# A four-layer graph network on one core: raw weight blocks loaded and turned first, and a landing wait inside the cell scatter

## The reference, cut to what matters

```python
# layer 0: mean of the neighbours, two 512x512 matrices, layernorm
h = x @ W_self.T + (segment_sum(x[src], dst) / deg) @ W_neigh.T + bias
# layer 1: two weighted graph convolutions (w = edge_weight, loops added)
# layer 2: a message per edge, then a GRU cell
m   = relu(concat(h[src], edge_attr) @ W1.T + b1) @ W2.T + b2
agg = segment_sum(m, dst)
gi, gh = agg @ W_ih.T + b_ih, h @ W_hh.T + b_hh      # 3 gates of 512 each
# layer 3: weighted sum of the neighbours, one matrix
x = x + segment_sum(h[src] * edge_w, dst) @ W.T + b
```

## Time and profile before

| | us |
|---|---|
| median of 3 runs | 1461.65 (1454.98 to 1465.86) |
| the profiled execution | 1465.06 |
| its span, first to last instruction | 1463.3 |
| first and last cell scatter issued on POOL | 42.82, 296.91 |
| PE: first transposes of the layer-0 tiles | 307.81 |
| SP: load of the sorted cells | 383.94 |
| PE: first matmul of the blocks | 391.82 |

### The profile page before, as it was taken

One profiled execution on the slowest core, in us unless ns is written; L12 is line 12 of the kernel. 1 busy time (PEld: TensorE's weight loads), 2 busy tenths in 40 slices (PEclk: granted clock), 3 DMA queues, 4 the chain that ended last, 5 costly groups with the idle time before them and its releaser, 6 DMA issues.

```text
span 1463.3 us, 20037 instructions
## 1 busy us (share of the span) xinstructions
PE 1204.0 (82%) x4298; PEld 748.8 (51%) x4298; DVE 1014.9 (69%) x2113; ACT 571.7 (39%) x1461; POOL 691.7 (47%) x760
## 2 busy tenths in 40 slices
PE   4410056579799999999999889999999999998998
PEld 1310023244344444455787655444444478887787
DVE  9750017645499999985237868888888889888543
ACT  0200011121377777022201128888887753334210
POOL 0577735710288888067667726666666500000000
PEclk9655568789899999999999999999999999999899
DMA  8811001511400000733422467777777600002220
GB/s 335 307 59 59 2 30 37 187 58 72 155 21 24 25 19 11 291 100 114 141 84 88 144 212 231 228 215 230 217 224 222 163 1 1 0 1 74 82 90 35
DMA packets 87258, 167.89 MB, mean 115 GB/s; under 512 B 16124, under 2 KB 44670, under 8 KB 84644
## 3 DMA queue, kind: packets, MB, share of 16 engines
q1 hardware_dynamic: 59588, 102.69, 20.8%
q0 software_dynamic: 25472, 59.97, 13.5%
q10 hardware_dynamic: 2144, 4.59, 1.0%
HBM read 115.96 MB, written 51.23 MB: 114 GB/s over the span
## 4 chain that ended last, share of the span: by engine, by line
PE 64%; DVE 12%; another core or an unknown queue 8%; issue 6%; DMA 3%; DVEq 2%; ACT 2%; POOL 2%; SPq 1%; ACTq 0%; POOLq 0%
PE pb L1328 10%; PE pb L1103 6%; PE pb L1228 6%; PE pb L1220 5%; PE pb L1423 5%; PE pb L1193 4%; PE pb L1396 4%; PE pb L1398 4%; PE pb L1397 4%; PE pb L1171 3%; PE pb L1342 3%; PE pb L1344 2%; PE pb L1345 2%; PE pb L1321 2%
## 5 line engine op out<-in xcount | busy, mean ns | idle before, releaser
L711 POOL DMA_INDIRECT cell_rows<-pay,idx x168 | 168.3, 1002 | 125.8 <-DVE idx L1569 74.5
L745 POOL DMA_INDIRECT dst_rows<-ering,gidx x168 | 172.4, 1026 | 100.8 <-issue 90.2
L1328 PE MATMUL pb<-arena 128*128 128x512 f32 x368 | 191.0, 602 | 13.0 <-ACT arena L970 12.5
L1113 PE MATMUL pb<-ident,arena 128*128 128x128 f32 x164 | 34.2, 382 | 132.6 <-issue 52.1
L799 POOL DMA_INDIRECT arena<-p_rows,arena x96 | 99.5, 1036 | 78.0 <-issue 26.9
L1897 DVE TENSOR_TENSOR arena<-pb,arena 128x512 f32<-128x512 f32 x184 | 122.1, 681 | 7.1 <-DMA arena<-p_rows,arena 3.7
L799 POOL DMA_INDIRECT arena<-p_rows,ws x88 | 92.6, 1052 | 50.7 <-issue 25.9
L1904 DVE SCALAR_TENSOR_TENSOR low<-arena,high 128x512 fp32r<-128x512 f32 x138 | 95.0, 688 | 29.2 <-ACT high L977 21.5
L855 ACT ACTIVATE arena<-iota,free 128x128 f32<-128x128 f32 x266 | 92.2, 394 | 53.3 <-PE pb L1193 39.5
L1540 DVE TENSOR_TENSOR arena<-pb,arena 128x505 f32<-128x505 f32 (+1 forms) x34 | 23.0, 677 | 126.3 <-remote 116.2
L813 ACT COPY ws<-pb 128x512 f32<-128x512 f32 x40 | 22.7, 589 | 224.5 <-remote 109.7
(11 more groups left out here) (329 smaller groups left out, 2663.0 us busy)
## 6 DMA issues: line engine op xcount, KB each, us to landing
dst_rows<-arena SPq DMA_DIRECT2D x6, 2046.0 KB, 17.5
ering<-in_edge_attr_dram SPq DMA_DIRECT2D x41, 256.0 KB
arena<-adj SPq DMA_DIRECT2D x10, 640.0 KB, 4.0
arena<-dst_rows SPq DMA_DIRECT2D x24, 264.0 KB
arena<-wt_gru SPq DMA_DIRECT2D x48, 128.0 KB
ws<-dst_rows SPq DMA_DIRECT2D x22, 264.0 KB
arena<-in_x_dram SPq DMA_DIRECT2D x18, 256.0 KB
arena<-in_L_gnn_W_hh_dram SPq DMA_DIRECT2D x3, 1024.0 KB
```

What stands on the lines that cost most here:

```text
L711: nc.gpsimd.indirect_dma_start(cell_rows[:, :], bass.IndirectOffsetOnAxis(idx1[:, j:j + 1], 0), pay1[:, j], None).then_inc(c_scattered[spa ...
L745: nc.gpsimd.indirect_dma_start(dst_rows[:, :], bass.IndirectOffsetOnAxis(gidx[:, k:k + 1], 0), ering[:, k, :], None).then_inc(e_scattered[ ...
L1328: nc.tensor.matmul(e_bank(k)[:], erowT[:, k % 4], w1e_sb, start=True, stop=True).then_inc(edge_mm, 1)
```

## The change

- SP loads the raw blocks before anything is zeroed. The zeros of `cell_rows` (two writes) follow the second block, those of `dst_rows` (24 writes of 512 KB instead of 6) follow the tenth. The zeros come from the edge ring `ering`, which DVE clears first (1056 elements a partition instead of 5120).
- The three turned "ih" blocks get places of their own (`ih_turned`) at the end of the adjacency area instead of sharing the ring `ws`. So PE turns all ten blocks first, between the counts and ranks, and multiplies in the second matrix (`fold`) after that. The x loads come behind all of it in SP's queue.
- In the cell scatter the first transfer of each span is issued as before; the second waits until all five transfers of the span before have landed. That is 33 added waits on POOL.
- DVE clears the adjacency area only after the last fold, and POOL and SP wait for the new counts of zero writes.

```diff
@@ -318,6 +319,12 @@
 
         ering_high = sb_under("ering_high", [P, 2, D], F32R)
         ering = sb("ering", [P, COL, EW])
+        zeros = ering[:].rearrange("p c w -> p (c w)")
+        CELL_ZEROS, DST_ZEROS = 2, 24
+        cell_zeros = (CELL_CHUNKS + SPARE) * 4 // CELL_ZEROS
+        dst_zeros = (DST_CHUNKS + SPARE) * EW // DST_ZEROS
+        assert max(cell_zeros, dst_zeros) <= COL * EW
+        assert cell_zeros * CELL_ZEROS == (CELL_CHUNKS + SPARE) * 4 and dst_zeros * DST_ZEROS == (DST_CHUNKS + SPARE) * EW
 
         assert over_rows + 9 * D <= vec2_start and low.shape[1] == (KT + 1) * D
         gru_high = [[ws_high[:, 0, k] for k in range(KT)],
...
@@ -452,6 +458,11 @@
         PARTS3 = numbered([("matrix", 0)] + [("row", k) for k in FIRST_ROWS] + [("matrix", 1), ("row", 9)]
                           + [("matrix", t) for t in range(2, NT)])
         wj = {b: A[("w", b, KT - 1 if b else 4)] + 1 for b in range(len(blocks))}
+        def turned_block(n):
+
+            name, third = blocks[n]
+            return ih_turned[:, third] if name[0:2] == "ih" else ws[:, n % 2]
+
         raw_src = {"w1h": w1_2, "ih0": w_ih, "ih1": w_ih, "ih2": w_ih, "hh0": w_hh, "hh1": w_hh,
                    "hh2": w_hh, "w3": w_3, "self": w_self, "neigh": w_neigh}
 
@@ -489,44 +500,40 @@
             column(wt_t, w_in, edges_loaded)
             column(w1t_t, w1_in.rearrange("e a -> (e a)"), edges_loaded)
 
-            sp.wait_ge(zero_ready, 1)
-            zc = (CELL_CHUNKS + SPARE) * 4
-            sp.dma_start(cell_rows.rearrange("(p c) w -> p (c w)", p=P), h.rearrange("p t d -> p (t d)")[:, 0:zc]).then_inc(cells_zeroed, 16)
-            for k in range(KT):
-                sp.dma_start(b2_col[:, k:k + 1], b2_2[k * P:(k + 1) * P].rearrange("(p a) -> p a", a=1)).then_inc(b2_loaded, 16)
-            zd = (DST_CHUNKS + SPARE) * EW
-            part = zd // 6
-            dz = dst_rows.rearrange("(p c) w -> p (c w)", p=P)
-            for k in range(6):
-                sp.dma_start(dz[:, k * part:(k + 1) * part], h.rearrange("p t d -> p (t d)")[:, 0:part]).then_inc(zeroed, 16)
-
             for n, (name, third) in enumerate(blocks):
-                if n == X_AFTER:
-                    sp.wait_ge(sorted_all, 1)
-                    sp.wait_ge(x_free, 1)
-                    for t in range(NT):
-                        m = P if t + 1 < NT else LAST
-                        sp.dma_start(xs[0:m, t], x_in[t * P:t * P + m, :]).then_inc(xe_loaded[t], 16)
                 if n >= 2:
                     sp.wait_ge(for_act, wj[n - 2])
                 wide = DE + D if name == "w1h" else D
                 raw = raw_src[name]
                 sp.dma_start(wst[:, n % 2, :, 0:wide],
                              raw[third * D:(third + 1) * D, :].rearrange("(o p) f -> p o f", p=P)).then_inc(raw_loaded[n % 2], 16)
-                if n == 3:
-                    sp.wait_ge(zeroed, 16 * 6)
+                if n == 1:
+                    sp.wait_ge(zero_ready, 1)
+                    cz = cell_rows.rearrange("(p c) w -> p (c w)", p=P)
+                    for k in range(CELL_ZEROS):
+                        sp.dma_start(cz[:, k * cell_zeros:(k + 1) * cell_zeros], zeros[:, 0:cell_zeros]).then_inc(cells_zeroed, 16)
+                    for k in range(KT):
+                        sp.dma_start(b2_col[:, k:k + 1], b2_2[k * P:(k + 1) * P].rearrange("(p a) -> p a", a=1)).then_inc(b2_loaded, 16)
+                if n == W2_AFTER:
                     sp.dma_start(w2_raw, w2_2.rearrange("(o p) f -> p o f", p=P)).then_inc(w2_loaded, 16)
                 if 1 <= n <= len(stored_blocks):
                     store_weights(sp, n - 1)
-                if n == len(blocks) - 1:
-                    sp.wait_ge(b2_ready, 1)
-                    for k, v in enumerate((b0, gamma0, beta0)):
-                        sp.dma_start(vec[:, k], v.rearrange("(a f) -> a f", a=1).to_broadcast([P, D])).then_inc(vec_loaded, 16)
-                if blocks[n - 2][0][0:2] == "ih":
-                    gate = blocks[n - 2][1]
-                    sp.wait_ge(act_read, A[("c", gate)] + 1)
-                    sp.dma_start(wt_dram[f"m{gate}"], m_out.rearrange("p k f -> p (k f)")).then_inc(m_stored, 16)
-                    sp.dma_start(c_dram[gate], c_out).then_inc(m_stored, 16)
+
+            dz = dst_rows.rearrange("(p c) w -> p (c w)", p=P)
+            for k in range(DST_ZEROS):
+                sp.dma_start(dz[:, k * dst_zeros:(k + 1) * dst_zeros], zeros[:, 0:dst_zeros]).then_inc(zeroed, 16)
+            sp.wait_ge(b2_ready, 1)
+            for k, v in enumerate((b0, gamma0, beta0)):
+                sp.dma_start(vec[:, k], v.rearrange("(a f) -> a f", a=1).to_broadcast([P, D])).then_inc(vec_loaded, 16)
+            for gate in range(3):
+                sp.wait_ge(act_read, A[("c", gate)] + 1)
+                sp.dma_start(wt_dram[f"m{gate}"], m_out.rearrange("p k f -> p (k f)")).then_inc(m_stored, 16)
+                sp.dma_start(c_dram[gate], c_out).then_inc(m_stored, 16)
+            sp.wait_ge(sorted_all, 1)
+            sp.wait_ge(x_free, 1)
+            for t in range(NT):
+                m = P if t + 1 < NT else LAST
+                sp.dma_start(xs[0:m, t], x_in[t * P:t * P + m, :]).then_inc(xe_loaded[t], 16)
 
             for t in range(1, NT + 2):
                 if t <= NT:
...
@@ -708,6 +717,9 @@
                 at_least(pool, c_scattered[span % 2], 16 * SPAN * (span // 2))
                 passed()
                 for j in range(SPAN * span, min(SPAN * span + SPAN, J)):
+                    if span and j == SPAN * span + 1:
+                        pool.wait_ge(c_scattered[(span - 1) % 2], 16 * SPAN * ((span + 1) // 2))
+                        passed()
                     nc.gpsimd.indirect_dma_start(cell_rows[:, :], bass.IndirectOffsetOnAxis(idx1[:, j:j + 1], 0),
                                                  pay1[:, j], None).then_inc(c_scattered[span % 2], 16)
 
...
@@ -822,26 +834,21 @@
             nc.scalar.copy(pay1[:, :, 3], w1t_t).then_inc(weights_copied, 1)
 
             for n in range(len(blocks)):
-                m = n - 2
-                if 0 <= m < len(stored_blocks):
+                m = {2: 0, 3: 1, 4: 2, 8: 4, 9: 3}.get(n)
+                if m is not None:
                     act.wait_ge(wt_stored[m % 2], 16 * (m // 2 + 1) + (16 if m % 2 == 0 else 0))
-                elif m >= 0:
-                    act.wait_ge(for_act, A[("c", blocks[m][1])] + 1)
-                if blocks[n][0] == "self":
-                    root(("he", 1), one_rstd[:])
                 for k in range(KT):
-                    copy_job(("w", n, k), ws[:, n % 2, k])
+                    copy_job(("w", n, k), turned_block(n)[:, k])
                 if n == 0:
                     copy_job(("w", 0, 4), tiles[:, 0])
-                if blocks[n][0] == "neigh":
-                    root(("he", 0), one_rstd[:])
-                if blocks[n - 1][0][0:2] == "ih":
-                    gate = blocks[n - 1][1]
-                    if gate:
-                        act.wait_ge(m_stored, 32 * gate)
-                    for k in range(KT):
-                        copy_job(("m", gate, k), m_out[:, k])
-                    copy_job(("c", gate), c_out)
+            for gate in range(3):
+                if gate:
+                    act.wait_ge(m_stored, 32 * gate)
+                for k in range(KT):
+                    copy_job(("m", gate, k), m_out[:, k])
+                copy_job(("c", gate), c_out)
+            root(("he", 0), one_rstd[:])
+            root(("he", 1), one_rstd[:])
 
             def flat(t4):
                 return t4.rearrange("p k n -> p (k n)")
@@ -1139,42 +1146,53 @@
                                            start=False, stop=g == last - 1)
                 ins.then_inc(for_dve, 1)
 
+            pe.wait_ge(const_ready, 8)
             pe.wait_ge(sort_const, 1)
             for q in range(len(O_PARTS) - 1):
+                if q < 2:
+                    turn_weights(q)
                 pe.wait_ge(hot1_ready, q + 1)
                 for g in range(O_PARTS[q], O_PARTS[q + 1]):
                     count_span(g)
-            pe.wait_ge(const_ready, 8)
+            turn_weights(2)
             pe.wait_ge(base_ready, 1)
-            for n in range(len(blocks)):
-                if n < 2:
-                    rank_spans(n)
-                elif n == 2:
-                    rank_spans(2)
-                    rank_spans(3)
-                elif n < 5:
-                    rank_spans(n + 1)
-                turn_weights(n)
-                if n == 6:
-                    rank_spans(6)
-                if blocks[n - 1][0][0:2] == "ih":
-
-                    gate = blocks[n - 1][1]
-                    pe.wait_ge(w2_loaded, 16)
-                    pe.wait_ge(b2_ready, 1)
-                    pe.wait_ge(act_read, wj[n - 1])
-                    for k in range(KT + 1):
-                        job = ("m", gate, k) if k < KT else ("c", gate)
```

(53 more changed lines are left out.)

22 lines of the change are left out of this document (11 added, 11 removed).

## The result

The changed kernel takes **1420.01 us** (median of 4, 1412.60 to 1420.17) against 1461.49 for the kernel before (4 runs), ratio 0.971, 95% interval 0.966 to 0.976. It is 41 us faster where 90 were forecast. The profiled execution took 1419.97, its span is 1418.2.

What follows compares the result with a forecast made beforehand. Bound: PE's late signals during POOL's unbroken cell scatter; afterwards the scatter itself. Scatter 257.7 + pauses 36 + handover 8 = 301.7 against 391.8, 90 us less, hence 1372 us; 8 in 10 for 1340 to 1430.

Steps and rivals of the forecast that it cites:

- These pauses ... let PE's signals through.: Cell scatter: pauses with no more than one transfer in flight let PE's signals through, as between edge scatters 1.52 us apart.
- Rival B: Pauses help halfway: PE gets one signal per span, about 7.3 us; tiles late, first matmul at 331, 1401 us; chance 12%.
- The main chain without late signals.: Sort, x load, layernorm, ten tiles: DVE's 86 us ends the sort near 129, PE starts about 157, chain ends near 231.
- The 33 pauses, 36 us.: POOL's landing waits: 6.4 pauses of 3.5 us under full DMA load plus 26.6 quiet ones of 0.5 us.
- The scatter as the bound at 294.: Cell scatter: 168 transfers at 1.287 us from 42.8 end at 257.7; with 36 us of pauses POOL stops near 294.
- Handover 8 us.: From the scatter's end through SP's load of the cells to the first block matmul: 6 plus 1.8 us for landing.
- Sum.: First block matmul at 257.7 + 36 + 8 = 301.7 against 391.8, 90 us less.
- Rival A: Zeros queued beside the scatter hold its landings, whole spans stand still: up to 22 us more, 1390 with 18; chance 12%.
- I take that as a fact of these rows: During a long unbroken scatter burst PE's signals reach the others late, about one in 11.1 us; mechanism left open.

Runs made afterwards that it cites:

- before_third: The kernel before, unchanged, run again in a session where PE's signals were prompt: 1324.98 us.
- after_third: The changed kernel, unchanged, run again in a session where PE's signals were prompt: 1370.59 us, ratio 1.033 to the kernel before.
- zeros_early: The changed kernel with its 24 zero writes right behind the column loads, in a session with prompt signals: 1377.20 us, ratio 1.035.
- order_only: The changed kernel without its landing wait, in a session with late signals: 1434.52 us, ratio 0.984 to the kernel before.
- gap_no_wait: The changed kernel with one small POOL memset per span in place of the landing wait, late signals: 1406.78 us, ratio 0.964.
- gap1: The changed kernel with one small POOL memset per span behind each landing wait, late signals: 1400.18 us, ratio 0.961.
- gap3_no_wait_b: The changed kernel with three POOL memsets per span in place of the landing wait, session with late signals: 1380.74 us, ratio 0.938.
- before_again: The kernel before, unchanged, run again in a later session with late signals: 1470.50 us.

## Why the prediction was wrong, step by step

- **"These pauses ... let PE's signals through."** This is the step that failed. It held for the sort (x at 140.79) and failed for the tiles. It rested on edge scatters 1.52 us apart, but the new quiet span takes 6.70 us, 1.34 per transfer, which is far nearer to the late 1.28 than to 1.52. The forecast's own figures, (6.43 + 0.5) / 5 = 1.39, already lay nearer to 1.28. The sort was saved by something else: beside the weight loads and zeros, until about 112 us, its pauses made spans of 10.9 to 13.5 us, 2.2 to 2.7 per transfer. Some 75 us after these ended the signals were late. The runs put 1.33 to 1.40 on the late side and 1.47 on the prompt side, and show that emptying the queue once in five transfers is not enough to let the signals through. Price: the first block matmul comes at 347.58 and not at the 313.20 of the same kernel with prompt signals, 34 us.
- **Rival B** comes nearest: the sort gets through and the tiles are late. Its price was too low (first matmul 331 for 347.6, 1401 for 1420). Its reason, "one signal per span", did not hold: the waits on remote grow from 3 to 41 us while the burst goes on.
- **The main chain without late signals.** x was forecast near 130 and is loaded at 140.79 (142.28 in before_third). DVE was taken as the bound with 86 us; from 45 to 141 us it is busy for 78. PE is busy for 75 of these 96 where 60 were counted, and ACT stands 18.47 and 5.04 us on "DMA c<-arena", the c store behind the 24 zero writes. With prompt signals the tiles are over at 254.18 in before_third and 244.66 in after_third, not at 231. None of this sets the end.
- **The 33 pauses, 36 us.** Measured 39: seven loaded ones with 32.5 us idle, less the usual 0.3 each, make 30.4 (22.4 forecast), and 26 quiet ones of 0.34 make 8.8 (13.3 forecast). The first five loaded pauses, 4.5 to 6.1 us, lie around the upper bound of 5.2 and not in the middle. That the sum came within 4 us is in part luck: the loaded part was 8 too low and the quiet part 4 too high. A quiet landing takes 2.57 + 0.34 = 2.9 us from the start of the issue. The Trainium skill ("DMA: Bandwidth & Descriptors", "Anatomy of one DMA — SWDGE (gpsimd) path") gives about 2.0 us plus bytes. This trace shows 2.9 from the start of POOL's issue, 1.9 from its end, and 8.7 from the start under load (2.57 + 6.1); the quiet pause of 0 that would follow from 2.0 did not come.
- **The scatter as the bound at 294.** 304.66: pauses 3 more, indices 2.3 us later instead of 1 earlier, and the rest mostly transfers that POOL issued more slowly, the two longest at 109.44 and 111.72 (1.98 and 3.67 us), beside two DVE operations of 2.08 and 4.01 us.
- **Handover 8 us.** 313.20 - 306.03 = 7.2 in the prompt trace.
- **Sum.** Of the 46 us by which the first matmul missed (347.6 for 301.7), 34 are late signals in the tile phase; the other 11.5 are the scatter's later end, less a handover shorter by 0.8.
- **Rival A** did not hold as described. No whole span stood still, and all pauses together are 3 us above the sum. The first two, 5.8 and 4.5 us, come before or just as the zeros start at 67.90, the next three beside them are 5.3, 5.2 and 6.1, and zeros_early has pauses of 3.5 to 4.6 with the zeros already landed. The zeros may add up to some 8 us in all (32.4 in zeros_early against 40.3 in after_third).
- **Not in the forecast at all:** that lateness comes and goes between sessions with the same kernel. "I take that as a fact of these rows" was true of one condition. Where it is absent the same change is 3.3% slower, by the very pauses that were priced at 36 us.

## What to carry to other kernels

A wait that no instruction in the program explains ("remote") may depend on the condition of the machine and not on the kernel alone: measure again in another session before a kernel is reordered around it, and judge a cure in both conditions. If such waits come with a long run of small indirect transfers, try spacing first: 1.1 us of filler per five transfers gained 6% where signals were late and cost 2% where they were not; the change itself gained 3% and cost 3%. And when a step rests on "a little apart is enough", put the new spacing beside the two spacings that the trace has and ask which it is nearer to.

## What the runs showed of the hardware

- In the late condition PE's signals to ACT and DVE come late while POOL issues the small indirect transfers of the cells without a break. Spacing and effect: 1.28 us (order_only), waits on remote over 4 us from 28 us after the first scatter and steps of about 11 us from 46; 1.33 (gap_no_wait), the same times, with steps of 8 to 11 us; 1.34 behind landing waits (the changed kernel), late some 75 us after the loaded pauses end, and growing; 1.35 to 1.40 (gap1), waits of up to 16.1 us; 1.47 in the mean (gap3_no_wait_b), none above 2.3. Another engine's signal is prompt in the same stretch: in the changed kernel, ACT's square root reaches DVE at 203.24 after a wait of 0.27 us.
- In the prompt condition the same 168 transfers 1.27 us apart delay nothing: none of its eleven traces has a wait on remote before 350 us.
- The recurrent stage differs too. Its 41 groups of weight loads, first and last, in before_again and in before_third:

```profile
866.48 3.77 SPq L640 DMA_DIRECT2D arena<-wt_gru  x8
...
1141.19 0.02 SPq L640 DMA_DIRECT2D arena<-wt_gru  x1
```
```profile
743.21 3.77 SPq L640 DMA_DIRECT2D arena<-wt_gru  x8
...
995.98 0.34 SPq L640 DMA_DIRECT2D arena<-wt_gru  x1
```

274.7 against 252.8 us, with POOL's gathers in it. So of the 145 us between the two conditions 123 lie ahead of the first block matmul and most of the rest here.
